# A three-branch graph-layer kernel: the experts' outputs, stored by slot and combined at the end, against added in DRAM to the nodes' rows tile by tile

## The chip, the cores and the metric

The kernel runs on one core of one Trainium2 chip. The metric is the device time of one execution in microseconds. Before the change the median of three runs is 2510.1 us (2508.7 to 2510.99).

## The reference, cut to what matters

The input is 1250 nodes of 512 numbers. Two branches, a four-layer graph attention and a kernelised attention block, are added to x; then comes a mixture of experts with a residual. Only the mixture is touched:

```python
h = xf @ shared_w1 + shared_b1
z = swiglu5(h, ...) @ shared_w2 + shared_b2
w, idx = jax.lax.top_k(softmax(xf @ gate_w + gate_b), K)       # K = 2 of E = 16 experts
w = w / jnp.sum(w, axis=-1, keepdims=True)
cw = sum over k of one_hot(idx) * w
he = einsum('nd,edh->enh', xf, expert_w1) + expert_b1          # hidden 2 * 384
oe = einsum('enh,ehd->end', swiglu5(he, ...), expert_w2) + expert_b2
y  = einsum('ne,end->nd', cw, oe)
out = x + y + z
```

Everything is float32. The experts' second biases, weighted by cw, are added in the shared branch, so each node's output row needs from the experts only two weighted rows of 512.

## The kernel before, in words

The mixture is the function `moe`, run last. Every engine has its own program; they meet at semaphores, and a program's order is the order of the code.

**Routing.** TensorE makes the gate logits (`gate_pe`, line 2272), VectorE picks two experts per node (`choose_dve`) and gives each of the 2500 (node, expert) choices a slot (`slots_dve`). Slots are grouped by expert in tiles of 64 (HALF); 54 tiles (SLOT_TILES) are the most there can be. GpSimd scatters every node's row twice into `slot_rows` in DRAM (line 2245), with one extra column behind the 512 that holds the place of its result; slots that no node takes stay zero (blank slots).

**Shared branch.** `shared_pe` does nine groups of matmuls (line 2440) with ScalarE and VectorE behind it; `shared_down_pe` (lines 2492, 2494) gives ten tiles of 125 nodes, which `shared_down_dve` adds to x (line 2502, semaphore s_added).

**Experts.** The 54 tiles are six streams of nine consecutive tiles (TURNS). A pair i takes the tile of two streams at once, one in the upper and one in the lower half of the partitions, so there are 27 pairs; three pairs make a turn. Streams' weights lie in six buffers (`ew1`, `ew2`). Consecutive tiles of a stream often have the same expert; then the gather of the next weights (`next_weights`, line 2682: one indirect DMA for w1, one for w2, for each stream) moves one row of 128 and leaves the others out by their index. Where the expert changes it moves all 128 rows: 1.57 MB of w1, 0.79 MB of w2. By the reference's own routing of these inputs (1044 of the 2500 choices are expert 2) 49 tiles are used, and the expert changes at 12 of the 48 hand-overs: in one stream behind pairs 2, 3, 5, 6, 7, 8, 22 and 23, in both behind pairs 4 and 11. The order of TensorE in iteration i of `experts_pe` is: first two thirds of the up product of pair i+1 (line 2582, 512 columns), turns of the gated values of pair i (line 2602), last third of pair i+1's up product (line 2582, 256 columns), turns of the slot rows of pair i+2 (line 2567), down product of pair i (line 2615). ScalarE copies the result out of psum into `h` (line 2673, out_made), over the buffer of the hidden values, of which there are three (SLOT_RING, `glu_dve`). GpSimd (`experts_pool`) has per pair two tiny operations on places (lines 2690, 2693), w1 gathers behind `up_mm`, w2 gathers behind `down_mm`, then the store of 128 rows to `slot_outputs` (line 2701). VectorE starts pair i's hidden values only when the store of pair i-3 has landed. SyncE loads biases and parameters for three pairs ahead and slot rows for ten pairs ahead.

**Combine.** When all stores have landed, SyncE and ScalarE load both results of every node back (tile `back`), VectorE multiplies them by the two weights and adds them to x (line 2732), and SyncE stores x to the output.

Of the kernel before, what the change touches and what calls it, by code (L numbers as in the profile page):

```python
# [8 lines left out]
F32 = mybir.dt.float32  # L9
# [2057 lines left out]
def moe(c, x, w_all, cols, rows, slot_dram, out):  # L2067
# [5 lines left out]

    nc, psum, ident, a = c.nc, c.psum, c.ident, c.a
# [8 lines left out]
    back_dram = nc.dram_tensor("slot_outputs", [2 * N + S * HALF, D], F32)  # L2083
    prm_in, gate_in, b2_in, w2_in, b1_in, prm_passed = c.sems("r_prm_in", "r_gate_in", "r_b2_in", "r_w2_in", "r_b1_in",
                                                              "r_prm_passed")
# [17 lines left out]
    stored = [c.sem(f"e_stored{u}") for u in range(U)]  # L2103
    place_made, slot_turned, x_made, up_mm, e_biased, e_clipped = c.sems(
        "e_place_made", "e_slot_turned", "e_x_made", "e_up_mm", "e_biased", "e_clipped")
    e_sig_made, e_glu_step, glu_made, turned, t_made = c.sems("e_sig_made", "e_glu_step", "e_glu_made", "e_turned",
                                                              "e_t_made")
    down_mm, out_made, added, out_stored = c.sems("e_down_mm", "e_out_made", "e_added", "e_out_stored")
    back_in = [c.sem(f"e_back_in{t}") for t in range(NT)]
    with ExitStack() as ctx:  # L2110
# [23 lines left out]
        lane = sb("m_lane", [P, EXPERTS])  # L2134
# [5 lines left out]
        ones = sb("m_ones", [P, 128])  # L2140
# [8 lines left out]
        slot_place = sb("m_slot_place", [128, PAIRS], I32)  # L2149
        place_of = sb("m_place_of", [P, 2, NT])  # L2150
        blank_place = sb("m_blank_place", [128, PAIRS])
# [8 lines left out]
        expert_f, same, weights_f = (x_flat[:, S * (EXPERTS + n):S * (EXPERTS + n + 1)] for n in range(3))  # L2160
# [21 lines left out]
        cols_flat = cols[0:P].rearrange("p c n -> p (c n)")  # L2182
        back = [(cols_flat[:, t * 2 * D:(t + 1) * 2 * D] if t < 4 else
                 w_flat[(t - 4) // 2][0:P, (t % 2) * 2 * D:(t % 2 + 1) * 2 * D]).rearrange("p (n d) -> p n d", n=2)
                for t in range(NT)]
        back_view = back_dram[0:2 * N, :].rearrange("(n t p) d -> t p n d", n=2, p=P)
# [9 lines left out]
        def route_sp():  # L2196
            sp = c.sp
            load(sp, gate_w[:], a["L0_ffn_gate_w"].rearrange("(p c) o -> p c o", p=128)).then_inc(gate_in, 16)
            load(sp, gate_b[:], a["L0_ffn_gate_b"].rearrange("(e n) -> e n", n=1)).then_inc(gate_in, 16)
# [14 lines left out]
        def route_pool():  # L2214
# [3 lines left out]
            g.iota(lane[:], [[1, EXPERTS]], base=0, channel_multiplier=0, **iota).then_inc(consts_made, 1)  # L2218
            g.iota(slot_id[:], [[1, S]], base=0, channel_multiplier=0, **iota).then_inc(consts_made, 1)
            g.iota(place_of[:], [[N, 2], [P, NT]], base=-2 * N, channel_multiplier=1, **iota).then_inc(consts_made, 1)  # L2220
            for e in range(2):
                g.wait_ge(consts_made, 3 + e)
                g.iota(blank_place[lanes(e)].rearrange("p (q s) -> p q s", s=SIDES),
                       [[HALF, TURNS], [2 * TURNS * HALF, SIDES]], base=2 * N + e * TURNS * HALF, channel_multiplier=1,
                       **iota).then_inc(consts_made, 1)
            g.wait_ge(consts_made, 5)
            g.iota(lane_of[:, 0:1], [[0, 1]], base=0, channel_multiplier=1, **iota).then_inc(consts_made, 1)
            g.memset(ones[:], 1.0).then_inc(consts_made, 1)
            g.memset(n_rows[:, :, D + 1:ROW], 0.0).then_inc(consts_made, 1)
            g.memset(before[:], 1.0).then_inc(consts_made, 1)  # L2230
            g.wait_ge(consts_made, 9)
# [7 lines left out]
            for n in range(2):  # L2239
                if n == 1:  # L2240
                    g.wait_ge(scattered, 16 * NT)
                g.tensor_tensor(n_rows[:, :, D], place_of[:, n, :], pos_f[:, n, :], ALU.subtract).then_inc(places_made, 1)
# [557 lines left out]
```

## Time and profile before

| what | value |
|---|---|
| time, median of three runs | 2510.1 us |
| the profiled execution: its own time | 2515.31 us |
| its span, first to last instruction | 2513.6 us |
| mean granted TensorE clock | 0.987 |
| experts' pairs, from the first slot turn to the last result | 2209.9 to 2482.1 us |
| load back, weigh, add, store (after the last result) | 2482.1 to 2513.6 us |

All times below are microseconds from the span's start unless marked otherwise. A row of a timeline gives start, duration, engine, line, operation, output and inputs, count, and in brackets the idle time ahead of it with what ended it.

### The profile page before, as it was taken

How to read it: one execution, taken by the hardware profiler on the slowest of the kernel's cores; microseconds unless marked ns; L12 is line 12 of the kernel's file. 1: busy time of each engine (PE TensorE's matmuls, PEld its weight loads, DVE VectorE, ACT ScalarE, POOL GpSimd, SP SyncE). 2: the span in 40 equal slices, each digit the busy share in tenths (PEclk: the TensorE clock that was granted, in tenths of full speed). 3: DMA queues.
4: the chain of work that ended last, by engine and by line, in shares of the span. 5: the costliest groups of instructions: out<-in, count | busy, mean ns of one | idle time of the engine just before them, and what ended most of it. 6: DMA issues, size and time to landing. Idle time of an engine off the chain costs nothing. (4 is left out here: it accounts for less than half of the span.)

```text
span 2513.6 us, 27154 instructions
## 1 busy us (share of the span) xinstructions
PE 2416.4 (96%) x9136; PEld 1361.7 (54%) x9136; DVE 1384.0 (55%) x2907; ACT 948.9 (38%) x1615; POOL 750.2 (30%) x1125
## 2 busy tenths in 40 slices
PE   8999999999999999999999999999999998998994
PEld 4565655444676555576555577555567653433341
DVE  7896760613876542776651577552387635333344
ACT  4885633211663120665211466211166312212221
POOL 2005102100653200564200264220075232334551
PEclk9999999999999999999999999999999999999997
DMA  5401001420665110566110266311166421769536
GB/s 161 134 23 36 33 29 38 121 81 17 155 155 151 26 38 1 126 155 170 37 55 1 72 158 155 93 27 38 25 158 161 117 66 51 230 237 320 173 101 204
DMA packets 134453, 259.56 MB, mean 103 GB/s; under 512 B 52521, under 2 KB 53001, under 8 KB 131975
## 3 DMA queue, kind: packets, MB, share of 16 engines
q1 hardware_dynamic: 87750, 152.10, 20.8%
q0 software_dynamic: 43824, 100.83, 14.9%
q10 hardware_dynamic: 2741, 4.89, 0.7%
q8 instruction: 74, 1.21, 0.2%
q14 instruction: 64, 0.52, 0.1%
HBM read 207.68 MB, written 27.34 MB: 94 GB/s over the span
## 5 line engine op out<-in xcount | busy, mean ns | idle before, releaser
L109 POOL DMA_DIRECT2D cols<-w x720 | 352.8, 498 | 849.0 <-DVE w L610 834.0
L410 PE MATMUL psum<-cols,w 128*128 128x500 f32 (+1 forms) x1120 | 393.3, 510 | 1.2 <-PEq L95 1.2
L490 PE MATMUL psum<-cols,rows 128*128 128x256 f32 (+1 forms) x1600 | 371.6, 380 | 8.3 <-DMA cols<-w 8.3
L670 ACT ACTIVATE g_prob<-g_prob,g_row_max 125x1250 f32<-125x1250 f32 x160 | 214.0, 1338 | 412.4 <-DVE g_row_max L597 412.4
L476 PE MATMUL psum<-g_k_cols,g_q_cols 128*125 128x512 f32 (+1 forms) x960 | 361.4, 513 | 3.3 <-DVE g_row_max L594 3.3
L490 PEld LDWEIGHTS psum<-cols,rows 128*128 128x128 f32 (+1 forms) x1600 | 304.6, 191 | 48.7 <-DMA cols<-w 9.7
L410 PEld LDWEIGHTS psum<-cols,w 128*128 128x128 f32 x1120 | 209.8, 189 | 173.2 <-issue 165.1
L594 DVE CUSTOM_DVE_ANT_0 g_prob<-psum,ln_count 125x1250 f32<-125x1250 f32 x160 | 233.6, 1460 | 116.7 <-PE psum L476 116.3
L476 PEld LDWEIGHTS psum<-g_k_cols,g_q_cols 128*125 128x125 f32 x960 | 179.3, 187 | 173.5 <-issue 161.1
L610 DVE STREAM_TRANSPOSE w<-g_prob 128x1280 f32<-128x1280 f32 x160 | 241.1, 1507 | 11.4 <-ACT g_prob L676 11.2
L676 ACT ACTIVATE g_prob<-g_prob,g_row_max 125x1250 f32<-125x1250 f32 x160 | 214.1, 1338 | 56.9 <-DVE g_row_max L584 56.9
L2582 PE MATMUL psum<-m_ew,m_x_cols 128*64 128x256 f32 (+1 forms) x576 | 156.4, 505 | 6.0 <-DMA cols<-in_L_ffn_expert_w,m_weights_of 5.8
L567 DVE TENSOR_SCALAR g_k_cols<-psum,g_bias_cols 128x500 f32<-128x500 f32 (+1 forms) x48 | 31.3, 652 | 228.6 <-PE psum L410 228.6
L503 PE MATMUL psum<-g_wo,g_q_cols 128*125 128x512 f32 x320 | 143.7, 593 | 1.8 <-ACT g_q_cols L682 1.8
L549 PE MATMUL psum<-w,g_k_cols 128*125 128x512 f32 x320 | 143.6, 592 | 0.0
L460 PE MATMUL psum<-w,cols 128*128 128x512 f32 (+1 forms) x320 | 139.3, 592 | 0.0
L2628 DVE TENSOR_TENSOR m_work<-psum,m_eb 128x768 f32<-128x768 f32 x27 | 41.0, 1517 | 155.6 <-PE psum L2582 155.6
L460 PEld LDWEIGHTS psum<-w,cols 128*128 128x128 f32 (+1 forms) x320 | 60.0, 187 | 71.7 <-issue 71.5
L1449 DVE TENSOR_SCALAR p_shared<-iota,p_edge_sum 125x250 f16<-125x250 f16 x334 | 96.9, 290 | 0.0
L2682 POOL DMA_INDIRECT m_ew<-in_L_ffn_expert_w,m_weights_of x64 | 64.2, 1004 | 108.1 <-PE psum L2615 58.2
L1447 DVE TENSOR_SCALAR p_shared<-iota,p_edge_sum 125x125 f16<-125x125 f16 x334 | 89.5, 268 | 9.3 <-PE psum L1480 9.1
L503 PEld LDWEIGHTS psum<-g_wo,g_q_cols 128*125 128x125 f32 x320 | 57.7, 187 | 64.1 <-issue 60.0
(345 smaller groups left out, 3261.7 us busy)
## 6 DMA issues: line engine op xcount, KB each, us to landing
cols<-w POOLq DMA_DIRECT2D x720, 80.0 KB, 3.3
cols<-w SPq DMA_DIRECT2D x560, 80.0 KB
m_eb<-in_L_ffn_expert_b SPq DMA_DIRECT2D x54, 192.0 KB, 5.7
w<-in_L_gnn_m_w SPq DMA_DIRECT2D x8, 1024.0 KB
slot_rows<-p_kf SPq DMA_DIRECT2D x1, 7128.0 KB, 32.4
rows<-slot_rows SPq DMA_DIRECT2D x54, 132.0 KB, 3.3
m_ew<-in_L_ffn_expert_w SPq DMA_DIRECT2D x4, 1536.0 KB, 11.8
w<-in_L_mix_W SPq DMA_DIRECT2D x4, 1024.0 KB, 5.0
```

The lines of the kernel that those rows point to most:

```text
L109: return eng.dma_start(out, in_, allow_slow_non_contiguous=True)
L410: ins = c.pe.matmul(c.bank(group_bank(g), width), wt[:, k, o * 128:(o + 1) * 128], y_cols[:, k, start:start + width], start=(k == 0), stop ...
L460: ins = pe.matmul(c.bank(V_BANKS[t], D, r), y_cols[:, k, t * 128:t * 128 + r], w[2][:, k, :], start=(k == 0), stop=(k == KC - 1))
L476: ins = pe.matmul(psum[0:P, at:at + width], q_cols[:, h, t * P:(t + 1) * P], k_cols[:, h, start:start + width], start=True, stop=True)
L490: ins = pe.matmul(c.bank(6 + g % 2, 256).rearrange("p (u a i) -> p u a i", u=2, a=SIDE), rows[0:r, j, h * 128:(h + 1) * 128], turned_keys[ ...
L503: ins = pe.matmul(c.bank(t % 2, D, P), q_cols[:, k, t * P:(t + 1) * P], wo[:, k, :], start=(k == 0), stop=(k == KC - 1))
L549: ins = pe.matmul(c.bank(t % 2, D, P), k_cols[:, k, t * P:(t + 1) * P], w[2][:, k, :], start=(k == 0), stop=(k == KC - 1))
L594: v.tensor_tensor_reduce(prob[0:P, u, 0:N], psum[0:P, at:at + N], ln_count[:, t, :], 1.0, NOT_AN_EDGE / 10, ALU.add, ALU.max, row_max[:, u ...
L610: v.transpose(square[s][:, :, u, :].rearrange("p b (j i) -> p b j i", i=SQUARE), prob_squares[u]).then_inc(squared, 1)
L670: s.activation(prob[0:P, u, 0:N], prob[0:P, u, 0:N], ACT.Exp, bias=row_max[:, u, 1:2], accum_out=row_max[:, u, 2:3]).then_inc(exp_made, 1)
L676: s.activation(prob[0:P, u, 0:N], prob[0:P, u, 0:N], ACT.Identity, scale=row_max[:, u, 3:4]).then_inc(prob_made, 1)
L2582: ins = pe.matmul(psum[lanes(e), at:at + cn], x_cols[u][:, k, lanes(e)], ew1[s][:, k, c0:c0 + cn], start=(k == 0), stop=(k == KC - 1))
```

## The change

Nine things change, all in `moe`.

1. `slot_outputs`, the store at line 2701 and the whole combine are gone. The shared branch's result is stored to the output rows right away: SyncE issues 20 stores (two for each tile) as `s_added` advances, ahead of the loads of streams 4's and 5's first weights.
2. ScalarE's copy out of psum multiplies each slot's row by its weight, which now travels in the slot rows (column 513); column 512 now carries the node's number plus one, 0 in a blank slot.
3. GpSimd adds each tile's 64 rows to the output in DRAM with an indirect DMA that accumulates (`add_outputs`). Two tiles may hold the same node, so each add waits until the one ahead of it has landed (semaphore `summed`): 54 adds in one chain. A hidden buffer is free when both adds of pair i-3 have landed.
4. Blank slots add zero, and must do so to rows that no other slot of their tile names. Such rows are found for each expert ("lent": `lent_dve`, `lent_pe`, `lent_tiles_dve`): 5 operations on VectorE behind group 5 of the shared branch and one in `slots_dve`, 16 matmuls of one column on TensorE behind group 7, 5 operations on VectorE between the last group and the first addition of line 2502.
5. SyncE loads column 512 of all slots in one DMA of 64x54 single numbers (`node_from`), ahead of stream 3's first weights; GpSimd turns it into the table of nodes with five small operations, and the tiny operations in each pair go.
6. The order in GpSimd's loop is now: w1 gathers for pair i, add of pair i-1's first tile, w2 gathers for pair i-1, add of its second tile.
7. TensorE turns the slot rows of pair i+2 right behind the gated values of pair i, ahead of the last third of pair i+1's up product.
8. Slot rows of pair i+10 are loaded behind `out_made` of pair i instead of behind its turns.
9. The gate matmuls wait for the gate weights alone and no longer for the gate bias as well.

The core of the diff:

```diff
+            for t in range(NT):
+                sp.wait_ge(s_added, t + 1)
+                load_tile(sp, out[t * P:(t + 1) * P, :], x[:, t, :], base_out)
             load_first_weights(4)
...
                 ins.then_inc(turned, 1)
+                if i + 2 < PAIRS:
+                    turn_slots_pe(i + 2)
                 if i + 1 < PAIRS:
                     up_pe(i + 1, BANK, 2 * FFN_I - BANK)
-                if i + 2 < PAIRS:
-                    turn_slots_pe(i + 2)
...
             if i >= U:
-                v.wait_ge(stored[u], 16 * (i // U))
+                v.wait_ge(summed, 32 * (i - U + 1))
...
-                s.copy(h[u][:, 0:D], c.bank(OUT)).then_inc(out_made, 1)
+                s.activation(h[u][:, 0:D], c.bank(OUT), ACT.Identity, scale=rows[:, i % R, D + 1:D + 2]).then_inc(out_made, 1)
...
+            def add_outputs(i, e):
+                j = tile_of(streams(i)[e], turn(i))
+                if i or e:
+                    g.wait_ge(summed, 16 * (2 * i + e))
+                g.indirect_dma_start(
+                    out=out[:, :], in_=h[i % U][lanes(e), 0:D], in_offset=None,
+                    out_offset=bass.IndirectOffsetOnAxis(ap=slot_node[:, j:j + 1], axis=0),
+                    compute_op=ALU.add).then_inc(summed, 16)
...
+            for i in range(PAIRS + 1):
+                if i < PAIRS and turn(i) + 1 < TURNS:
                     g.wait_ge(up_mm, i + 1)
                     next_weights(i, ew1, w1_rows, next_w1_in)
+                if i == 1:
+                    g.wait_ge(base_out, 32 * NT)
+                if i >= 1:
+                    g.wait_ge(out_made, i)
+                    add_outputs(i - 1, 0)
+                    if turn(i - 1) + 1 < TURNS:
+                        g.wait_ge(down_mm, i)
+                        next_weights(i - 1, ew2, w2_rows, next_w2_in)
+                    add_outputs(i - 1, 1)
+            g.wait_ge(summed, 32 * PAIRS)
...
+            for e in range(EXPERTS):
+                at = OUT * BANK + e
+                ins = pe.matmul(psum[0:HALF, at:at + 1], lent_hot[:, e, :], lane_of[0:HALF, 0:1], start=True, stop=True)
```

GpSimd's queue in one pair before (a store, two operations on places, w1 gathers of 3072 numbers a row, w2 gathers of 1536, the next store):

```order
L2701 DMA slot_outputs<-m_work,m_slot_place 5956x512
L2690 TENSOR_TENSOR m_blank_place<-rows,m_blank_place 128x1
L2693 CAST m_slot_place<-m_blank_place 128x1
L2682 DMA w<-in_L_ffn_expert_w,m_weights_of 128x3072
L2682 DMA m_ew<-in_L_ffn_expert_w,m_weights_of 128x3072
L2682 DMA w<-in_L_ffn_expert_w,m_weights_of 128x1536
L2682 DMA m_ew<-in_L_ffn_expert_w,m_weights_of 128x1536
L2701 DMA slot_outputs<-m_work,m_slot_place 5956x512
```

The same queue in the changed kernel, in one iteration and the start of the next (lines are those of the changed kernel):

```order
L2731 DMA m_ew<-in_L_ffn_expert_w,m_weights_of 128x3072
L2731 DMA cols<-in_L_ffn_expert_w,m_weights_of 128x3072
L2740 DMA out<-m_work,m_slot_node 1250x512
L2731 DMA m_ew<-in_L_ffn_expert_w,m_weights_of 128x1536 x2
L2740 DMA out<-m_work,m_slot_node 1250x512
L2731 DMA w<-in_L_ffn_expert_w,m_weights_of 128x3072
L2731 DMA m_ew<-in_L_ffn_expert_w,m_weights_of 128x3072
L2740 DMA out<-m_work,m_slot_node 1250x512
```

One store has become two adds with the w2 gathers between them, and the w1 gathers of a pair stand one pair earlier against the results.

TensorE in one pair before (turns of gated values, last third of the next up product, turns of slot rows, down product):

```order
L2582 MATMUL psum<-m_ew,m_x_cols 64x512 x8
L2602 MATMUL psum<-ident,m_work 128x128 x3
L2582 MATMUL psum<-m_ew,m_x_cols 64x256 x8
L2567 MATMUL psum<-ident,rows 128x128 x4
L2615 MATMUL psum<-w,m_t_cols 64x512
```

and in the changed kernel:

```order
L2632 MATMUL psum<-m_ew,m_x_cols 64x512 x8
L2652 MATMUL psum<-ident,m_work 128x128 x3
L2617 MATMUL psum<-ident,rows 128x128 x4
L2632 MATMUL psum<-m_ew,m_x_cols 64x256 x8
L2664 MATMUL psum<-w,m_t_cols 64x512
```

The four turns of slot rows moved ahead of the eight matmuls of 256 columns; nothing else of the pair moved.

TensorE near the end of the shared branch in the changed kernel (the groups, now line 2483, with the turns of cw, and the lent matmuls):

```order
L2483 MATMUL psum<-cols,w 128x250 x8
L2460 MATMUL psum<-ident,m_cw 16x125 x2
L2483 MATMUL psum<-cols,w 128x250 x8
L2358 MATMUL psum<-m_lane_of,m_x_cols 64x1 x16
L2483 MATMUL psum<-cols,w 128x250 x8
L2540 MATMUL psum<-w,m_ew 125x512 x3
```

The 16 matmuls of one column stand between the eighth group and the ninth; nothing stands there before.

## Rows read from the trace of the kernel before

**Rows 1.** The page: busy time of each engine over the span.
```profile
PE 2416.4 (96%) x9136; PEld 1361.7 (54%) x9136; DVE 1384.0 (55%) x2907; ACT 948.9 (38%) x1615; POOL 750.2 (30%) x1125
```

**Rows 2.** Busy time by stretch, PE to POOL; last: clock, DMA share, GB/s.
```profile
2209.90:2482.10 272.20, 255.19 (x1377) 102.65 (x1377) 99.17 (x135) 61.04 (x108) 133.15 (x174) 0.96 0.62 202
2243.00:2322.00 79.00, 70.44 (x373) 28.23 (x373) 28.12 (x38) 16.84 (x30) 39.83 (x51) 0.94 1.01 323
2425.00:2434.00 9.00, 9.00 (x53) 3.62 (x51) 3.70 (x5) 2.27 (x4) 5.33 (x8) 1.00 0.29 79
```

**Rows 3.** The chain that ended last, one pair of the experts.
```profile
2429.48 3.43 PE psum L2582 x16
2432.91 0.48 PE psum L2602 x3
2433.39 1.88 PE psum L2582 x16
2435.27 0.59 PE psum L2567 x4
2435.85 2.73 PE psum L2615 x12
```

**Rows 4.** Timeline after the last down product.
```profile
2481.46 0.59 ACT L2673 COPY m_work<-psum 128x512 f32<-128x512 f32 x1 [4.59 <-PE psum L2615]
2482.80 0.99 POOL L2701 DMA_INDIRECT slot_outputs<-m_work,m_slot_place  x1 [5.67 <-ACT m_work L2673]
...
2493.58 16.49 SPq L109 DMA_DIRECT2D out<-xbuf  x20
```

**Rows 5.** Landing times of the stores (line 2701): 2480:2490, 2425:2434, 2270:2279.
```profile
DMA to landing us min/median/max: 2.7/2.7/2.7
...
DMA to landing us min/median/max: 3.6/3.6/3.6
...
DMA to landing us min/median/max: 19.0/19.0/19.0
```

**Rows 6.** Landing times of the weight gathers (line 2682) in 2425:2434.
```profile
DMA to landing us min/median/max: 2.4/2.8/3.1
```

**Rows 7.** Timeline of GpSimd, one pair.
```profile
2431.58 0.99 POOL L2682 DMA_INDIRECT m_ew<-in_L_ffn_expert_w,m_weights_of  x1 [0.30 <-issue]
2432.87 1.04 POOL L2701 DMA_INDIRECT slot_outputs<-m_work,m_slot_place  x1 [0.30 <-issue]
...
2434.95 1.03 POOL L2682 DMA_INDIRECT m_ew<-in_L_ffn_expert_w,m_weights_of  x1 [0.57 <-issue]
```

**Rows 8.** Timeline of TensorE, its waits for w1 weights in the pairs.
```profile
2279.53 1.09 PE L2582 MATMUL psum<-m_ew,m_x_cols 128*64 128x512 f32 x1 [5.75 <-DMA cols<-in_L_ffn_expert_w,m_weights_of]
...
2293.44 1.09 PE L2582 MATMUL psum<-w,m_x_cols 128*64 128x512 f32 x1 [2.81 <-DMA m_ew<-in_L_ffn_expert_w,m_weights_of]
...
2323.99 0.61 PE L2582 MATMUL psum<-w,m_x_cols 128*64 128x512 f32 x1 [1.28 <-DMA m_ew<-in_L_ffn_expert_w,m_weights_of]
...
2354.76 1.00 PE L2582 MATMUL psum<-w,m_x_cols 128*64 128x512 f32 x1 [3.25 <-DMA m_ew<-in_L_ffn_expert_w,m_weights_of]
```

**Rows 9.** The chain that ended last, gate and shared branch.
```profile
2101.22 3.27 DMA m_gate_b<-in_L_ffn_gate_b
...
2162.00 6.77 PE psum L2440 x32
```

**Rows 10.** Weight loads of TensorE in 2209.9:2482.1, grouped by line.
```profile
L2582 PEld LDWEIGHTS psum<-m_ew,m_x_cols 128*64 128x64 f32 x576 | 59.2, 140 | 60.4 <-issue 51.9 <-ACT m_x_cols L2645 0.5
```

**Rows 11.** First weights of stream 5: timeline of its loads, landing times.
```profile
2211.34 0.85 SPq L109 DMA_DIRECT2D m_ew<-in_L_ffn_expert_w  x2
...
DMA to landing us min/median/max: 10.6/11.2/11.9
```

**Rows 12.** Timeline of VectorE: 864 elements of 128 partitions; one addition of line 2502.
```profile
2126.42 1.05 DVE L2364 TENSOR_TENSOR m_x_cols<-m_tiles_of,m_slot_id 128x864 f32<-128x864 f32 x1
...
2182.30 0.69 DVE L2502 TENSOR_TENSOR xbuf<-xbuf,psum 125x512 f32<-125x512 f32 x1 [3.13 <-PE psum L2494]
```

More of the change, by code:

```diff
@@ L2159, in moe @@
         passed = x_flat[:, 0:S * EXPERTS].rearrange("p (s e) -> p s e", e=EXPERTS)
[L2160 removed]
+        lent_hot = x_flat[0:HALF, 0:EXPERTS * HALF].rearrange("p (e n) -> p e n", e=EXPERTS)
+        lent_pick = x_flat[0:HALF, 0:S * (EXPERTS + 1)].rearrange("p (s e) -> p s e", e=EXPERTS + 1)
+        expert_f, expert_in, same, weights_f = (x_flat[:, 1024 + n * S:1024 + (n + 1) * S] for n in range(4))
+        ones = x_flat[0:P, 1280:1408]
+        lent_lane = x_flat[0:HALF, 1408:1408 + HALF]
+        lent_at, one_tile = (x_flat[0:HALF, 1472 + n * EXPERTS:1472 + (n + 1) * EXPERTS] for n in range(2))
         turned_logit = x_all[0:EXPERTS].rearrange("p u c n -> p (u c n)")[:, 0:N]
@@ L2699, in experts_pool @@
-                g.wait_ge(place_made, 2 * i + 2)
-                g.wait_ge(out_made, i + 1)
-                g.indirect_dma_start(
-                    out=back_dram[:, :], in_=h[i % U][:, 0:D], in_offset=None,
-                    out_offset=bass.IndirectOffsetOnAxis(ap=slot_place[:, i:i + 1], axis=0)).then_inc(stored[i % U], 16)
-        def wait_stored(eng):
-            for u in range(U):
-                eng.wait_ge(stored[u], 16 * len(range(u, PAIRS, U)))
-        def combine_act():
-            s = c.act
-            wait_stored(s)
-            for t in range(1, NT, 2):
-                load_tile(s, back[t], back_view[t], back_in[t])
@@ L2715, in combine_sp @@
-        def combine_sp():
-            sp = c.sp
-            wait_stored(sp)
-            for t in range(0, NT, 2):
-                load_tile(sp, back[t], back_view[t], back_in[t])
-            for t in range(NT):
-                sp.wait_ge(added, 2 * (t + 1))
-                load_tile(sp, out[t * P:(t + 1) * P, :], x[:, t, :], out_stored)
-            sp.wait_ge(out_stored, 32 * NT)
-        def combine_dve():
-            v = c.dve
-            for t in range(NT):
-                v.wait_ge(back_in[t], 32)
-                for n in range(2):
-                    if n == 1:
-                        v.wait_ge(added, 2 * t + 1)
-                    v.scalar_tensor_tensor(x[:, t, :], back[t][:, n, :], weight[:, t, n:n + 1], x[:, t, :], ALU.mult,
-                                           ALU.add).then_inc(added, 1)
+                if i == 1:
+                    g.wait_ge(base_out, 32 * NT)
```

144 lines of the change are left out of this document (86 added, 58 removed).

## The prediction

> **What bounds the kernel now.** The page's first part says that TensorE is busy in 96% of the span [rows 1]; the change touches the mixture of experts alone, so the next view is busy time by stretch. In the pairs (2209.90 to 2482.10) TensorE works 255.19 of 272.20 us [rows 2]. The chain of waits shows one pair there as TensorE alone: 3.43 + 0.48 + 1.88 + 0.59 + 2.73 = 9.11 us [rows 3]. Its waits are four, all for a w1 gather: 5.75 + 2.81 + 1.28 + 3.25 = 13.1 us [rows 8]. The first three lie where the DMA share is 1.01 and 323 GB/s move [rows 2]. Behind the last result TensorE is done: that result is out of psum at 2481.46 + 0.59 = 2482.05, the last store starts at 2482.80 [rows 4], lands 2.7 us later [rows 5], and loading back, weighing and storing take until the span's end at 2513.6. The last output stores are issued from 2493.58 on for 16.49 us [rows 4].
>
> **The tail: what goes and what comes.** From 2482.05 to 2513.6 are 31.55 us, and all of it goes, because the base of the output has long been stored. What comes is two adds in a row. I need the landing of an add, which no row shows. From below: a store of twice the rows lands in 2.7 us when nothing else runs, and half the bytes can only shorten that. From above: a destination that must first be read costs at most one more whole trip, and a gather of one row takes 2.4 [rows 6], so 2.7 + 2.4 = 5.1. The two trips share the issue of about 1.0 us, and only the way out of the read is new; I take 3.2, near the store. Result to issue is 0.75 (2482.05 to 2482.80), a freed GpSimd restarts after 0.3 [rows 7]. Alone the tail is 0.75 + 3.2 + 0.3 + 3.2 = 7.5. The chain of adds will not be quite up to date there: pairs 22 and 23 each hand over one real set of weights, and the last pair is shorter than 9.11. I add 3. Term: -31.5 + 10.5 = **-21** (ends: 6 to 20 us of tail, -25.5 to -11.5).
>
> The Trainium skill, "DMA: Bandwidth & Descriptors", section Anatomy of one DMA, gives 2.0 us plus bytes over 436 GB/s, which is 2.3 for 131 KB, and has no term for reading the destination. By it the tail would be 0.9 + 0.9 shorter than with my 3.2; the store's row (2.7, against 2.6 by the page) agrees for plain stores and says nothing of adds.
>
> **The pairs, lightly loaded.** A chain of 54 adds has to keep pace with TensorE. In light traffic the store lands in 3.6 instead of 2.7 (79 GB/s, share 0.29) [rows 2, 5]; so I raise the add by the same 0.9, to 4.1. Two adds a pair are then 2 x (4.1 + 0.3) = 8.8 us against TensorE's 9.11: they keep up with 0.3 to spare. GpSimd itself issues six DMAs a pair at 1.3 us each (2431.58, 2432.87) = 7.8, and the 1.3 us of place operations (2433.9 to 2434.95) go [rows 7]; the w2 gathers stand between the two adds and fill that wait. Term: **0** (ends: 0, and with an add at 5.1 + 0.9 = 6.0 us, 2 x 6.3 - 9.1 = 3.5 us a pair).
>
> **The pairs, DMA full.** One real hand-over is 2.36 MB. What 323 GB/s leave beside the light traffic of 79 is 244 GB/s, so it takes 9.7 us; eight of them behind pairs 2 to 8 need 77 us in 7 x 9.1 = 64 us of TensorE, 13 too many. That is about the 9.8 us of waits there now. The change issues w1 earlier: now the gathers of a pair start after the pair's predecessor is stored (2434.95, while the columns they wait for were done before 2429.48), then at once, some 8 us sooner [rows 3, 7]. That could take all 13.1 us of waits. But the adds stand in the same queue behind real weights: there the store lands in 19.0 us [rows 5], and nothing waits for it yet. The hidden buffer is wanted 9.11 + 3.43 + 0.48 + 1.88 = 14.9 us after the down product, 14.3 after the result [rows 3]: enough for two adds of 4.4, not for two behind weights, up to 38 in the worst pair. Then VectorE waits for the buffer, and TensorE for VectorE. The bytes are the same, plus the adds' reads; so I expect the wait to come back in another name, and a little longer, since each add that waits holds back the w1 gathers behind it. Term: from 13.1 to about 20, **+7** (ends: -13 if the adds slip through, +25 if the worst pairs pay the full 38).
>
> **What is added ahead of the pairs.** The lent matmuls are 16 in the program; TensorE is the chain there (6.77 us for groups eight and nine with nothing between) [rows 9]. In the trace each float32 product counts twice (x16 in [rows 3] where the program's order has x8), and a weight load of 64 columns is 140 ns [rows 10]: 32 x 0.14 = 4.5. Lower end: each counts once, 2.2; upper end: load and product not overlapped at all, 9. Term **+4.5**. The gate matmuls wait for a bias load issued at 2101.22 and landed 3.27 later [rows 9]; the weights' load goes out one issue earlier, 0.4 us. Term **-0.4** (0 to -2).
>
> **Edits at nothing.** VectorE's five lent operations behind group 5, and five before line 2502, of which four go over 864 to 1024 numbers at 1.05 and up: about 2 and 3.5 us. TensorE takes 0.69 + 3.13 = 3.8 us for a tile of the shared down product [rows 12], so the first tile hides them, with four psum banks behind it; without that cover they would cost 3.5. The 20 base stores and the 64x54 load on SyncE: they push streams 4's and 5's first weights back by 1 to 2 us; stream 5's land 11.9 after 2211.34 [rows 11], thus 2223.2; pair 2's product comes behind pair 0's up product and the first iteration, 2209.9 + 5.3 + 9.1 = 2224.3 at the earliest, and later by pair 0's hidden values. That is thin cover; gone, it costs 1 to 3 us once. Slot turns ahead of the 256 columns: the five pieces of a pair only change places; hidden values start 0.59 later, but VectorE and ScalarE work 3.70 and 2.27 of 9.00 us [rows 2], 3 us to spare even were they one chain. ScalarE's scale: same form as its copy. Slot rows are loaded ten pairs ahead; 6 us later is nothing.
>
> **Sum.** -21 + 0 + 7 + 4.5 - 0.4 = -9.9. Against the profiled execution's own 2515.31 this is 2505.4; that execution is 5.2 above the median of the runs, so I say 2500.
>
> **The rivals.** (a) *The chain of adds becomes the bound (slower).* It decides when an add plus restart passes 4.55 us, half a pair: my value is 4.4, so it is near. Priced at 5.0 landed, 5.3 with restart: 10.6 a pair, 27 pairs from the first result at about 2229 are 286 us, end at 2515; the full stretch adds its 20 and the lent matmuls 4.5: 2540 in the span, 2535 as a time. For it: everything is serial, and 19.0 us in the full stretch. Against: the 3.6 us of twice the rows in light traffic.
> The Trainium skill, same page, section Latency and other measured facts, gives memory access as 0.2 us on average and "2 µs at high load"; by that an add's extra read would be 2 us in this stretch, landing 5 and more, and this rival would hold. No row here shows a read-modify-write.
> (b) *Given back.* The adds keep up in light traffic, but the full stretch costs 15 us more than I took: about 2513. For it: both adds of pairs 4 to 8 stand behind weights.
> (c) *w1's head start pays.* The waits of 13.1 go and do not return: -21 - 13 + 4 = -30, about 2480. Against: the DMA share there is already 1.01, and 77 us do not fit into 64 by issuing sooner, except for what pairs 0 and 1 leave idle.
>
> **How the numbers follow.** Forecast case, 2490 to 2507: 0.54. (a) 2518 to 2600: 0.24. (b) 2507 to 2518: 0.15. (c) 2478 to 2488: 0.07. The range from 2486 to 2538 leaves out most of (c) and the upper part of (a). 0.2% of 2510 is 5 us, about what a measurement of this kernel can tell from no change: faster is below 2505.1, which takes 0.50 of the forecast case and all of (c), 0.57; within, 2505.1 to 2515.1, has 0.04 of it and 0.09 of (b), 0.13; slower 0.30. The sign rests on (a) more than on anything else, and the likeliest case's own range is 2490 to 2507.
>
> **What would show it.** Right: the span ends 7 to 14 us behind the last result, with no load back; the adds land in about 4.1 us in light traffic and over 10 in the full stretch; TensorE's waits for w1 go and VectorE waits at the hidden values (the operation from psum and m_eb) for the adds; between the eighth and ninth group of the shared branch stand some 4.5 us; a lightly loaded pair still takes 9.11. Wrong: pairs of 10 us and more in light traffic mean (a); a landing under 3 us there would make the tail 6 and me too high. If GpSimd's issue of an add takes much more than 1.0 us, its own queue (7.8 of 9.11) becomes the limit before the landings do.

## The result, and the profile after

The changed kernel takes 2533.01 us (median of 4 runs, 2530.9 to 2536.53) against 2509.4 of the kernel before beside it: ratio 1.0095, 95% interval 1.0077 to 1.0112. It is slower by 24 us, where 2500 was forecast. Its profiled execution took 2530.9 us, with a span of 2529.2.

The page of the changed kernel: busy time of the engines, VectorE's first operation on the hidden values, and the adds (count, busy us and mean ns, idle time ahead and what ended most of it).

```profile
PE 2419.5 (96%) x9168; PEld 1369.6 (54%) x9168; DVE 1372.5 (54%) x2898; ACT 947.7 (37%) x1615; POOL 795.9 (31%) x1102
...
L2677 DVE TENSOR_TENSOR m_work<-psum,m_eb 128x768 f32<-128x768 f32 x27 | 40.6, 1502 | 182.5 <-DMA out<-m_work,m_slot_node 134.8
...
L2740 POOL DMA_INDIRECT out<-m_work,m_slot_node x54 | 78.5, 1453 | 88.1 <-DMA out<-m_work,m_slot_node 71.1
```

TensorE's work is what it was [rows 1]; VectorE now waits 134.8 us and GpSimd 71.1 us for the landing of adds, and an add takes GpSimd 1.45 us where the store took 1.04 [rows 7].

The ruler for all runs is the start of ScalarE's copy of each pair's result (line 2722 here, 2673 before). The first and the last of the changed kernel, from ScalarE's timeline:

```profile
2230.80 0.67 ACT L2722 ACTIVATE m_work<-psum,rows 128x512 f32<-128x512 f32 x1
...
2509.04 0.69 ACT L2722 ACTIVATE m_work<-psum,rows 128x512 f32<-128x512 f32 x1 [4.22 <-PE psum L2664]
```

From these stamps comes this table, in us; the last column is from the last stamp to the span's end:

| kernel | first result | pairs 0 to 3 | 3 to 14 (real weights) | 14 to 22 (light) | 22 to 26 | end |
|---|---|---|---|---|---|---|
| before | 2228.32 | 27.30 | 119.30 | 72.80 | 33.74 | 32.14 |
| changed | 2230.80 | 26.80 | 137.59 | 74.34 | 39.51 | 20.16 |
| difference | +2.5 | -0.5 | **+18.3** | +1.5 | **+5.8** | **-12.0** |

Together +15.6, the difference of the spans. The times differ by 24: the profiled execution of the kernel before took 2515.31 us, 5.9 above the median beside it, that of the changed kernel 2.1 below its own. So 8 us of the slowdown stand in no column, and the columns are good to a few us.

Busy time by stretch (PE to POOL, clock, DMA share, GB/s): pairs 3 to 14 of the kernel before, then pairs 3 to 14, 14 to 22 and 22 to 26 of the changed kernel:

```profile
2255.62:2374.92 119.30, 106.21 (x563) 42.60 (x561) 40.22 (x56) 24.95 (x44) 59.69 (x77) 0.94 0.83 268
...
2257.60:2395.20 137.60, 110.80 (x565) 47.70 (x563) 39.58 (x55) 24.50 (x46) 76.50 (x66) 0.90 0.82 232
2395.20:2469.50 74.30, 72.10 (x416) 30.97 (x414) 29.00 (x40) 17.70 (x33) 56.45 (x49) 1.00 0.47 94
2469.50:2509.00 39.50, 30.21 (x154) 12.21 (x150) 12.01 (x17) 7.31 (x14) 18.83 (x16) 0.91 0.56 144
```

In the window of [rows 2] that had 323 GB/s (2243 to 2322) the DMA engines now move 283, at a share of 0.95 for 1.01; over pairs 3 to 14 it is 232 for 268, at 0.82 for 0.83. TensorE's idle time there doubles, from 13.1 to 26.8 us, and its work, 106.21 before, takes 110.80 at a granted clock of 0.90 for 0.94. The bytes of the stretch are the same, 32 MB in either kernel, and take longer, so bytes alone do not explain the wait. The chain that ended last runs there through GpSimd and the adds alone, from 2285 to 2309:

```profile
2285.22 0.36 POOL out L2740
2285.58 1.40 issue
2286.98 1.02 POOL m_ew L2731
...
2288.31 0.78 POOL cols L2731
...
2289.70 8.13 DMA out<-m_work,m_slot_node
...
2298.63 0.36 POOL out L2740
2298.99 1.40 issue
2300.39 1.02 POOL w L2731
...
2303.14 6.02 DMA out<-m_work,m_slot_node
```

An add, two gathers, the next add; this one lands 8.13 us after its issue, 6.02 in the next round. That add stands right behind gathers of real weights. In light traffic (GpSimd's timeline) the steps from add to add are 4.69, 4.52 and 4.66 us:

```profile
2426.04 1.45 POOL L2740 DMA_INDIRECT out<-m_work,m_slot_node  x1 [0.30 <-issue]
2427.80 1.02 POOL L2731 DMA_INDIRECT m_ew<-in_L_ffn_expert_w,m_weights_of  x1 [0.30 <-issue]
2429.13 0.99 POOL L2731 DMA_INDIRECT m_ew<-in_L_ffn_expert_w,m_weights_of  x1 [0.30 <-issue]
2430.73 1.45 POOL L2740 DMA_INDIRECT out<-m_work,m_slot_node  x1 [0.61 <-PE psum L2664]
...
2435.25 1.45 POOL L2740 DMA_INDIRECT out<-m_work,m_slot_node  x1 [0.30 <-issue]
...
2439.91 1.45 POOL L2740 DMA_INDIRECT out<-m_work,m_slot_node  x1 [0.58 <-PE psum L2664]
```

Here the chain runs through GpSimd's issues, one behind the other, from 2421 to 2470, and only once through the landing of an add, which takes 4.26 us:

```profile
2448.83 0.34 POOL out L2740
2449.17 1.41 issue
2450.59 1.02 POOL m_ew L2731
...
2453.34 4.26 DMA out<-m_work,m_slot_node
```

The end, where nothing else runs (the chain): the adds are behind, and four are worked off in a row, one every 4.1 us.

```profile
2508.53 3.76 DMA out<-m_work,m_slot_node
...
2512.56 3.52 DMA out<-m_work,m_slot_node
...
2516.83 3.61 DMA out<-m_work,m_slot_node
...
2520.71 1.40 POOL out L2740
```

### The profile page after: what moved, and what is told of

The parts are those of the page before. It is cut to its first block and busy times, and to the rows that moved or that the text cites. A ratio compares the mean times of both kernels' runs of the same rounds, so it can differ in the third digit from the quotient of the medians.

```text
span 2529.2 us, 27151 instructions
## 1 busy us (share of the span) xinstructions
PE 2419.5 (96%) x9168; PEld 1369.6 (54%) x9168; DVE 1372.5 (54%) x2898; ACT 947.7 (37%) x1615; POOL 795.9 (31%) x1102
## 5 line engine op out<-in xcount | busy, mean ns | idle before, releaser
L2632 PE MATMUL psum<-m_ew,m_x_cols 128*64 128x256 f32 (+1 forms) x576 | 162.2, 525 | 0.3 <-ACT m_x_cols L2694 0.3
L2677 DVE TENSOR_TENSOR m_work<-psum,m_eb 128x768 f32<-128x768 f32 x27 | 40.6, 1502 | 182.5 <-DMA out<-m_work,m_slot_node 134.8
L2740 POOL DMA_INDIRECT out<-m_work,m_slot_node x54 | 78.5, 1453 | 88.1 <-DMA out<-m_work,m_slot_node 71.1
L2632 PEld LDWEIGHTS psum<-m_ew,m_x_cols 128*64 128x64 f32 x576 | 62.5, 148 | 56.4 <-issue 49.6
```

What stands on the lines that cost most here:

```text
L2632: ins = pe.matmul(psum[lanes(e), at:at + cn], x_cols[u][:, k, lanes(e)], ew1[s][:, k, c0:c0 + cn], start=(k == 0), stop=(k == KC - 1))
```

## The experiments

Times are medians; "before" is the kernel before on the same chip. Stretches are those of the table.

**1. Slot turns alone.** The kernel before with edit 7 only.

```diff
+                if i + 2 < PAIRS:
+                    turn_slots_pe(i + 2)
                 if i + 1 < PAIRS:
                     up_pe(i + 1, BANK, 2 * FFN_I - BANK)
-                if i + 2 < PAIRS:
-                    turn_slots_pe(i + 2)
```

> The kernel before with edit 7 alone: slot turns of pair i+2 right behind the gated values' turns. My step says it is worth nothing: the pair stays 9.11 us, VectorE starts 0.59 us later with about 3 us to spare. Expected ratio to before 0.999 to 1.001 (2508 to 2512 us). The rival, that the later end of the up product holds VectorE or GpSimd's gathers back, would show as pairs over 9.11 us and +5 us or more.

2511.98 against 2509.15, ratio 1.0003 (0.9988 to 1.0017). No change in the time, yet not nothing in the trace: pairs 14 to 22 take 71.06 us, not 72.80. Experiment 10 takes this up.

**2. Early w1 gathers alone.** The kernel before with pair i+1's w1 gathers ahead of pair i's w2 gathers and store.

```diff
-                    g.wait_ge(up_mm, i + 1)
-                    next_weights(i, ew1, w1_rows, next_w1_in)
+                if i + 1 < PAIRS and turn(i + 1) + 1 < TURNS:
+                    g.wait_ge(up_mm, i + 2)
+                    next_weights(i + 1, ew1, w1_rows, next_w1_in)
```

> The kernel before, with the w1 gathers of pair i+1 issued ahead of pair i's w2 gathers and store, as in the changed kernel, and nothing else. If the head start of some 8 us pays by itself (my case c), TensorE's 13.1 us of waits for w1 shrink to under 5: 2500 to 2503 us. If the full DMA stretch sets them (two loads' worth of bytes in the time of fewer pairs), the waits stay at 9 or more: 2507 to 2511.

2502.46, ratio 0.9974 (0.996 to 0.9988): TensorE has no wait for w1 left, and pairs 3 to 14 take 108.60 instead of 119.30. So the head start that the change brings is worth 7 us in the time and 11 in this stretch of the trace by itself; in the changed kernel the same stretch takes 137.59.

**3. A ring of ten for the results.** In the changed kernel the result is written over its slot row, so that VectorE needs no add to have landed.

```diff
-                s.activation(h[u][:, 0:D], c.bank(OUT), ACT.Identity, scale=rows[:, i % R, D + 1:D + 2]).then_inc(out_made, 1)
+                s.activation(rows[:, i % R, 0:D], c.bank(OUT), ACT.Identity, scale=rows[:, i % R, D + 1:D + 2]).then_inc(out_made, 1)
...
-                sp.wait_ge(out_made, i - R + 1)
+                sp.wait_ge(summed, 32 * (i - R + 1))
...
-                v.wait_ge(summed, 32 * (i - U + 1))
```

> The changed kernel, with the weighted result written over the slot row it came from (ten buffers instead of three), the adds reading there, so VectorE no longer waits for adds; slot rows of pair i+10 wait for the adds of pair i. Theory A (VectorE's wait for the hidden buffer is what costs in the full stretch): its 135 us of waits go, pairs there return to about 10, time falls by 10 to 20 us, to 2513 to 2523. Theory B (the chain of 54 adds on GpSimd is itself longer than TensorE's work, and holds the weights' gathers behind it): the wait moves to TensorE's w1 gathers and to the tail, and the time stays within 5 us of the changed kernel, 2528 to 2538.

2533.89, ratio to before 1.0099 (1.0074 to 1.0125). But VectorE's waits had only changed their name; its waits in this run:

```profile
DVE m_work L2675 <- DMA m_eprm<-swiglu_params: 86.2, 10, 12.8
```

SyncE loads an expert's parameters behind its new wait for the adds. This run did not settle it; number 12 repeats it without that.

**4. Two chains.** The second tile's adds go to a second array (its sums are missing from the output), each chain with its own semaphore.

```diff
-                if i or e:
-                    g.wait_ge(summed, 16 * (2 * i + e))
+                if i:
+                    g.wait_ge(chain[e], 16 * i)
...
-                    out=out[:, :], in_=h[i % U][lanes(e), 0:D], in_offset=None,
+                    out=(out, out2)[e][:, :], in_=h[i % U][lanes(e), 0:D], in_offset=None,
```

> The changed kernel, with the adds of a pair's second tile going to a second, uninitialised array in DRAM, so that there are two chains of 27 adds and no add waits for the other tile's; the second array is left out of the output (that part of the result is missing). Same issues, same bytes. Theory B (one chain of 54) expects the chain to be no bound any more: pairs of 11.5 us in the full stretch fall to about 10, tail from 19.5 to about 12, in all 20 to 30 us less than the changed kernel, 2503 to 2513. Theory C (adds cost by their bytes, reads of the destination, and by GpSimd's issue of 1.75 us each) expects under 5 us of change.

2498.28, ratio 0.9964 (0.9947 to 0.998): 35 us below the changed kernel with the same adds, bytes and issues. Pairs 3 to 14 take 116.57, 22 to 26 33.08, the end 10.88. It is more than the 20 to 30 of Theory B. The edit takes away the wait of each add for the one ahead and brings in the second array. The array is no rival: in the changed kernel no two adds are under way together, so they cannot hinder each other in the one array. The wait is the cause of the loss.

**5. The adds without adding.**

```diff
-                    out_offset=bass.IndirectOffsetOnAxis(ap=slot_node[:, j:j + 1], axis=0),
-                    compute_op=ALU.add).then_inc(summed, 16)
+                    out_offset=bass.IndirectOffsetOnAxis(ap=slot_node[:, j:j + 1], axis=0)).then_inc(summed, 16)
```

> The changed kernel with the accumulation left out: each indirect DMA writes its 64 rows over the output rows instead of adding to them; order and waits as they are (the sums are left out of the output). Theory A (the accumulation itself is dear: a longer issue on GpSimd and a longer landing, because the destination is read first): the issue falls from 1.45 us to about 1.0, the step of the serial chain in the unloaded tail from 4.0 us to about 3.0, the pairs of the full stretch by 1 us and more, and the time by 12 to 22 us, to 2511 to 2521. Theory B (only the serial waits behind weights and the one chain cost, whatever the DMA does): steps and issue stay, the time stays within 5 us of 2533.

2503.52, ratio 0.9976 (0.9965 to 0.9987): 29.5 us below the changed kernel, more than either theory said. The issue is 0.93 us (median of 54) instead of 1.45. Its end, in the chain that ended last:

```profile
2484.40 2.58 DMA out<-m_work,m_slot_node
...
2490.59 2.60 DMA out<-m_work,m_slot_node
...
2493.45 0.90 POOL out L2740
```

The last five steps there take (2493.45 - 2477.84) / 5 = 3.12 us each, in the changed kernel (2520.71 - 2500.39) / 5 = 4.06. So accumulating costs 0.94 us an add unloaded, half in the issue and half behind it. Paid 54 times that would be 51 us; 29.5 of them show, since TensorE is the bound in part of the pairs: light pairs are 8.80 (pairs 17 to 23). Pairs 3 to 14 take 125.73, pairs 14 to 22 68.86, and the end is 12.03. No run tells apart what the longer issue costs and what the longer landing does.

**6. Half the adds.**

```diff
             def add_outputs(i, e):
+                if e:
+                    return
```

> The changed kernel with the second tile's add of every pair left out (its rows are missing from the output): one chain of 27 adds, and five DMAs a pair in GpSimd's queue instead of six. The two-chain run had lightly loaded pairs of 9.29 us on average and no long waits for landings there. Theory A (in light traffic GpSimd's own queue of six issues is what makes 9.2 to 9.3 us of 9.11): the light pair is 9.11 again, pairs 14 to 22 take 72.8 us instead of 74.3, and the time is 3 to 8 us below the two-chain kernel's 2498, about 2492. Theory B (something else holds the light pairs): they stay at 9.2 to 9.3 and the time is within 3 us of 2498.

2478.13, ratio 0.9873 (0.9856 to 0.989), 14 below Theory A's figure: light pairs are 8.80, not 9.11, and pairs 3 to 14 take 107.06. Pairs 14 to 22 (70.41) equal those of experiment 9, which has all six issues, so Theory A's reason fell: see there. Each chain of experiment 4 has 27 adds too, and that kernel is 20 us slower: so much do the other 27 adds cost by being issued and moved.

**7 and 8. No real hand-over.** One comparison is changed in both kernels, so that every gather moves one row.

```diff
-            v.tensor_tensor(same[:, 1:], expert_in[:, 1:], expert_in[:, 0:S - 1], ALU.is_equal).then_inc(step, 1)
+            v.tensor_tensor(same[:, 1:], expert_in[:, 1:], expert_in[:, 0:S - 1], ALU.is_ge).then_inc(step, 1)
```

> The kernel before with every hand-over of weights reduced to the one row that unchanged experts move (the new experts' weights are left out, so tiles behind a change are computed with old weights): issues and order as before, the bytes gone. The intervals between results of pairs 3 to 14 have 19 us over 9.1 a pair now; all of it should go: about 2491. It is the base for the same edit in the changed kernel.

> The changed kernel with the same reduction of every hand-over to one row (new experts' weights left out). Theory A (the loss comes where adds stand behind real weights; in light traffic the adds about keep up): it is faster than the kernel before with the same reduction, by 5 to 15 us: -12 or better for the tail (nearer -18, since there is no lag to work off), +2.5 ahead of the pairs, +0.1 to 0.2 us for each of 27 pairs; about 2480. Theory B (two serial adds and four gathers a pair are too much for the chain whatever the load): pairs of 9.5 us and more, and the changed kernel is slower than its twin, 2495 and more.

2492.31 and 2484.37: without the bytes the changed kernel is 8 us faster than its twin. Here TensorE is never idle in pairs 3 to 14, and they take 100.11 in the one and 96.80 in the other (busy time by stretch). The twin of the kernel before:

```profile
2253.00:2354.00 101.00, 101.00 (x567) 41.08 (x565) 41.22 (x56) 25.36 (x46) 60.05 (x77) 1.00 0.38 107
```

The changed kernel's:

```profile
2257.00:2354.00 97.00, 97.00 (x565) 42.08 (x563) 41.35 (x56) 24.57 (x45) 76.39 (x66) 1.00 0.54 111
```

With the bytes it is 24 slower: adds and real weights in each other's way are worth 32 us. In pairs 3 to 14 of the changed kernel the bytes cost 40.8 us (137.59 against 96.80), of which TensorE is idle for 26.8 and works longer for 14.0 (110.80 against 96.80) at a granted clock of 0.90 instead of 1.00.

Without the bytes the adds are still a little too slow. The steps from add to add are 4.5 us on average up to pair 13 (2232.34 to 2352.90 in 27 steps), 8.9 a pair against TensorE's 8.80; VectorE waits 51.1 us for adds in this trace, from pair 18 to 22 a pair takes 9.2 to 9.3, and the end is 19.33 us, 13 shorter than the twin's 32.38 and not the 18 of Theory A.

**9. Two chains, made whole.** As 4, with the second array filled with zeros long before and merged at the end.

```diff
+            g.dma_start(out=out[:, :], in_=out2[:, :], accum_op=ALU.add, max_dma_last_dim=8192).then_inc(summed, 16)
```

> The two-chain kernel made whole: the second array is filled with zeros long before, and at the end one accumulating DMA on GpSimd's queue adds its 1250 rows to the output. All outputs are there. Without the merge it took 2498. The merge reads 2.56 MB twice and writes it once; at the 190 to 280 GB/s that the late stretches of these kernels move, 7.7 MB take 27 us if reads and writes count alike, 13 if the second read and the write lie beside the first read: 2511 to 2528, so faster than the changed kernel (2533), and not faster than the kernel before with the early w1 gathers (2502).

2506.77, ratio 0.9985 (0.9976 to 0.9995): a whole kernel with adds that is 26 us faster than the changed one, and 4 below the range expected. Its end is 26.77 us, 16 longer than in 4; its pairs were 9 us quicker in the profiled execution, of which 4 in light traffic (70.40 against 74.28). Why those of 4 were slower with the same issues stays open. GpSimd's timeline in its light stretch has adds at 2395.33, 2399.71, 2404.10 and 2408.48, every idle time before an instruction 0.30 or 0.31: six issues take 2 x 4.38 = 8.77 us, and TensorE's pair is 8.80. So six issues just fit. The steps of 4.5 to 4.7 us in the changed kernel are three such issues, of which a gather often takes 1.14 instead of 0.99, and 0.3 to 0.7 us more ahead of each pair's first add. The trace puts that rest down to the down product; but the add's own result is out of psum over 6 us earlier by then, and the one other thing that it waits for is the landing of the add ahead. That this is it is not shown.

**10. The early w1 gathers with the gate wait, without and with the slot turns.** The diffs of 2 and, for the second kernel, of 1; in both

```diff
-            pe.wait_ge(gate_in, 32)
+            pe.wait_ge(gate_w_in, 16)
```

> The same without the slot turns' move: early w1 gathers and the gate wait alone. 2502.5 - 1.5 = 2501; the difference to the kernel with the turns moved is 5 us by Theory A and under 2 by Theory B.

> The kernel before with three edits: w1 gathers ahead of the pair's w2 gathers (2502.5 alone), the gate products waiting for the gate weights only (1.5 us earlier at the first group in the changed kernel's trace), and the slot turns right behind the gated values' turns (lightly loaded pairs of 8.80 instead of 9.10 us in the traces that have them). Theory A (the turns' 0.30 us a pair counts once w1 is not waited for): 17 or more undisturbed pairs give 5 us: about 2496. Theory B (as in the run with the turns alone, it is given back in waits): about 2501.

2502.05 (0.9962 to 0.9985) and 2497.16 (0.9943 to 0.997). The gate wait is worth nothing (2502.46 without it); the slot turns are worth 4.9 us once TensorE has no w1 to wait for, though the two intervals overlap a little; the traces bear it out with 70.39 against 72.81 us for pairs 14 to 22. One pair of the kernel with them, the chain:

```profile
2403.25 3.43 PE psum L2582 x16
2406.68 0.48 PE psum L2602 x3
2407.16 0.44 PE psum L2567 x4
2407.59 1.88 PE psum L2582 x16
2409.47 2.57 PE psum L2615 x11
```

Beside [rows 3] the slot turns take 0.44 instead of 0.59 next to the other turns, the down product 2.57 instead of 2.73: a pair is 8.80. This kernel beats both.

**11. Lent matmuls behind the ninth group.**

```diff
-                if n == LENT_AFTER:
-                    lent_pe()
+            lent_pe()
```

> The changed kernel with the 16 lent matmuls of one column behind the ninth group of the shared branch instead of behind the eighth, so that they fall into the 1.97 us in which TensorE waits for the last hidden values. In the changed kernel they take 1.95 us, and the ninth group behind them 5.28 instead of 3.38 us at a granted clock of 0.68. Theory A (the low clock is what 32 one-column products leave behind, and the group behind them pays): the ninth group is 3.38 us again at clock 1.00, the lent matmuls lie in a wait, and the first products of the shared down part may run slowly in its place; from the start of group eight to the first result, between 2 and 3.9 us are won. Theory B (the low clock comes from something else at that time, such as the transfers then): the ninth group stays at 5.3 us and about 2 us are won. Time 2529 to 2531 by both, since the adds still set the end.

2531.07 (2526.76 to 2539.26), not told apart from 2533.01. In the trace the edit wins what it can. The changed kernel's chain at that place:

```profile
2164.09 1.95 PE psum L2358 x32
2166.04 5.28 PE psum L2483 x16
```

Its busy time microsecond by microsecond, where the third number from the right is the granted clock:

```profile
2165.00:2166.00 1.00, 1.00 (x19) 0.98 (x18) 0.96 (x3) 0.17 (x1) 0.70 (x2) 1.00 0.29 51
2166.00:2167.00 1.00, 1.00 (x4) 0.86 (x4) 0.20 (x1) 0.00 (x0) 0.74 (x1) 0.62 0.61 159
2167.00:2168.00 1.00, 1.00 (x3) 0.77 (x3) 0.00 (x0) 0.00 (x0) 0.95 (x1) 0.50 0.41 106
```

Behind 32 products of one column the granted clock falls to 0.50, the 1.2 GHz level, though TensorE was busy all the time, and 16 matmuls take 5.28 us instead of 3.38. Moved, they lie in the wait for the last hidden values, with nothing slower behind them:

```profile
2161.54 6.76 PE psum L2483 x32
2168.30 1.95 PE psum L2358 x32
2170.25 0.03 issue
2170.28 2.84 PE psum L2539 x6
```

From the start of group eight to the first slot turns it is 47.9 us (2161.54 to 2209.41) instead of 51.7 (2160.70 to 2212.41): the whole 3.85. Theory A held.

The fall does not always hit the ninth group. With the lent matmuls in the old place those 16 matmuls take 5.28 us in three traces (the changed kernel, 4 and 12) and 3.59 in five (3, 5, 6, 8 and 9). In these five the fall comes later: the ninth group is followed by the wait of 1.97 us for hidden values, and the first six products of the down part then take 4.54 us (4.39 in 8) instead of 2.84. The chain of experiment 3 there, and a microsecond of its busy time, with a granted clock of 0.50:

```profile
2172.40 4.54 PE psum L2540 x6
...
2174.00:2175.00 1.00, 1.00 (x3) 0.48 (x2) 0.96 (x2) 0.00 (x0) 0.69 (x2) 0.50 0.69 178
```

From group eight to the first slot turns all eight traces have 51.7 us. The kernel before has the same wait without the lent matmuls and takes 47.9, with nothing slower behind it: what the lent matmuls cost is 3.85 us in every trace.

Another fall of the clock (0.51 in 2214 to 2216 of the changed kernel) moves the first result: the first up products take 7.1 us in the traces of the kernel before, the changed one, 2, 4, 8, 11 and 12, and 5.41 in 1, 3, 5, 6, 7, 9 and both of 10. First results of two traces can differ by these 1.7 us alone.

**12. The ring again, with SyncE free.** As 3, with the slot rows asked for four pairs later, behind the biases that the pairs need.

```diff
-                if i + R < PAIRS:
-                    load_slots(i + R)
+                if i >= 4 and i - 4 + R < PAIRS:
+                    load_slots(i - 4 + R)
```

> The run with the result written over its slot row (ring of ten) took VectorE's wait for the adds away but put one on SyncE, whose loads of biases and parameters stand behind it: VectorE waited 86 us for those in its place. Here SyncE asks for the slot rows four pairs later, so that the adds may lag about seven pairs before anything but GpSimd waits for them. Theory A (the loss is VectorE's wait for hidden buffers, so more buffers would cure it): TensorE's pairs of the full stretch fall to those of the kernel before, the last result comes about 20 us earlier, and the time is near 2515. Theory B (GpSimd's own program is the bound: it issues, waits for landings in its place in the queue, and the w1 gathers stand behind those waits): VectorE's waits go to TensorE's for w1 or to the end, where the adds still to do are worked off after the last result; the time stays at 2528 to 2536.

2529.94, ratio 1.0082 (1.0056 to 1.0109). Waits of TensorE, VectorE and GpSimd from 2210 on:

```profile
PE psum L2632 <- DMA m_ew<-in_L_ffn_expert_w,m_weights_of: 16.1, 4, 10.6
PE psum L2632 <- DMA cols<-in_L_ffn_expert_w,m_weights_of: 13.0, 5, 5.5
...
DVE m_work L2675 <- PE psum L2632: 171.7, 27, 18.4
...
POOL out L2738 <- DMA out<-rows,m_slot_node: 74.7, 28, 8.7
```

VectorE no longer waits for any add. Instead TensorE waits 29.1 us for w1 (in the changed kernel once, 2.6), and after the last result (2501.13) 28.07 us remain, with adds still being issued at 2521.16. Pairs 3 to 14 take 128.85, 8.7 less than in the changed kernel, and the end takes 7.9 more. Theory B held: the bound is GpSimd's program. GpSimd's waits for landings are as they were (74.7 and 71.1), but that sum prices nothing: it is 74.0 in experiment 5, which is 29.5 us faster. Not tested is a kernel in which the weight gathers do not stand behind the waits for adds, so how much the chain of adds costs by its own length and how much by holding back the gathers stays open.

## Why the prediction was wrong

**The step that failed** is the one that carries the sign: that the adds keep pace with TensorE ("they keep up with 0.3 to spare") and that only a short wait comes back where the DMA is full. With the wait of each add for the one ahead taken away, 35 us of the time go (experiment 4). Rival (a) happened, the chain of adds as the bound, but distributed otherwise than it was worked out: hardly in light traffic, mostly in the full stretch as in rival (b), and in the tail. That its 2535 lies beside 2533.01 is luck: it had 10.6 us for each of 27 pairs, where the full stretch has 12.5 and the light one 9.3.

- **Price of an add.** Forecast 3.2 alone, measured 3.5 to 3.8; restart 0.3, measured 0.27 within a pair and 0.76 between pairs; issue 1.0, measured 1.45. In light traffic 4.1 was forecast for the landing, and the one landing that the chain shows there took 4.26. "Near the store" was too low, by the 0.94 us a step that accumulating costs. With plain scatters in the same place the kernel takes 2503.5 (experiment 5) and the terms come out near the forecast: pairs 3 to 14 +6.4 for +7, the end -20.1 for -21. So the design was priced as if an add were a store.
- **Pairs, lightly loaded: 0.** Measured +1.5 over pairs 14 to 22. The sum compared two adds of 4.4 with a TensorE pair of 9.11. With the slot turns moved, which is edit 7 of the same change, the pair is 8.80: by the forecast's own numbers nothing was to spare, and the bound of rival (a) was 4.40 and not 4.55. The change lost 3.9 us there against what it could have had. What holds these pairs is GpSimd's issues, 8.77 us for the six and not 7.8, as the last sentence of "What would show it" said.
- **Pairs, DMA full: +7.** Measured +18.3, inside the ends. I had the w1 waits going (13.1 to 2.6) and VectorE's wait coming, and both came; I took that wait for the cost. Experiment 12 shows that it is only where the cost appears. The 19.0 us of the store were not what adds paid (6 to 9), but most steps paid something. And TensorE's work in this stretch takes 4.6 us more at the lower clock, though the moved slot turns make it 3.3 shorter (96.80 against 100.11 in 8 and 7); the sum had no such term. The cost is that an add behind real weights lands after 6 to 9 us, and that GpSimd waits for it with all that stands behind it in its program; with two chains the stretch takes 21 us less.
- **Pairs 22 to 26: 3 of lag.** Measured +5.8 in the pairs, and more in the tail: the last pair's first add starts 7.1 us after its result is out (2509.73 to 2516.83), where I had 3.75.
- **Tail: -21.** Measured -12. Besides the lag (3.4) the two adds take 0.8 more, and 4.9 us pass from the last landing (about 2524.3, by 3.6 behind the last issue) to the span's end. I had nothing there. The old tail had less of it: its last bytes moved at about 2512, 1.4 us before the span's end, those of the changed kernel at about 2524, 5 us before. No row shows what passes in that time, and why it is longer stays open.
- **Lent matmuls: +4.5.** Measured 3.85 in all eight traces, but the size is near by luck: the 32 records take 1.95 us, 0.061 each and not the 0.14 of a weight load, and 1.9 are the clock that falls behind them, which I did not have.
- **Gate wait: -0.4.** The gate products start 2.1 us earlier and run slower (11.43 us for 10.81), so the first group starts 1.5 earlier; in experiment 10 that does not show in the time.
- **Slips that change nothing.** The operations on places and the gap between them are 1.04 us in [rows 7], not 1.3. Rival (b), 15 above the forecast, is 2515, not 2513.
- **At nothing.** The lent operations on VectorE and the base stores are hidden, as said: the ten shared down tiles still follow each other every 3.82 us. The slot turns are not nothing (0.30 us a pair), though alone they give no time (experiment 1).

The Trainium skill, "DMA: Bandwidth & Descriptors", section Latency and other measured facts, was quoted for 0.2 us of memory access on average and 2 at high load. Of the unloaded 0.94 us that accumulating costs, half is in the issue; the other half lies between these two. The step of 8.93 us in the full stretch (2289.70 to 2298.63) is far above both; it belongs to the weights ahead of the add, since without the bytes no step is longer than 5.71 (experiment 8). The same page, section Rules for kernel authors, says of accumulating DMAs that the destination is read and written later with nothing holding the bytes in between, so that an earlier add must be waited for by its semaphore. No run here left such a wait out; where the waits are fewer (4, 9) the adds go to different arrays.

## What to carry to other kernels

A serial chain of DMAs is priced at its landing under the load that stands in the same queue, not alone: multiply landing plus restart by the chain's length first, and compare it with the pace of the pair that the rest of the change makes. The issues of the same program are a second sum beside it: here they alone were 8.77 of 8.80 us. If the chain's waits stand in the program of the engine that also issues the weights, more buffers do not help (experiment 12); two independent chains with a merge do (26 us here). When a wait vanishes from one engine in an experiment, look on which engine it came back before calling the resource free.

## What was not expected of the hardware

- An accumulating indirect DMA of 64 rows of 2 KB: issue 1.45 us against 0.93 for the plain one, step in a serial chain 4.06 against 3.12.
- TensorE's granted clock fell to 0.50 behind 32 records of one-column products in eight of eight traces: in three at once, with the engine busy throughout, in five one group and a wait of 1.97 us later. The cost to the first slot turns was 3.85 us in each. With the products directly ahead of the down part (one trace) it did not fall there.
- Four transposes directly behind three others took 0.44 us instead of 0.59, and the down product, which then no longer follows transposes, 2.57 instead of 2.73.
- A merge of 2.56 MB in DRAM by one accumulating DMA lengthened the end by 16 us, where 13 to 27 were estimated.
